# Routed gate and up products with the expert's weights as the stationary operand

## The reference, cut to what matters

```python
gu = einsum('th,ehf->etf', x, w_gate_up)      # per expert 512 -> 2 x 256
act = silu(gate) * up                         # 256
eo = einsum('eti,eih->eth', act, w_down)      # 256 -> 512
routed = einsum('te,eth->th', combine, eo)    # weights of the two chosen experts
```

## Time and profile before

| | us |
|---|---|
| median of 3 runs (range) | 1273.26 (1271.31 to 1275.28) |
| the profiled execution's own time | 1275.16 |
| its span from first to last instruction | 1273.4 |
| PE busy | 1205.0 (95%), mean granted clock 0.986 |
| PEld busy | 816.2 (64%) |
| DVE / ACT / POOL busy | 661.2 / 475.8 / 491.4 |
| DMA | 217.40 MB moved |

### The profile page before, as it was taken

The page is one execution under the profiler, slowest core; times in us unless marked ns, Lnnn a source line. Parts: engine busy times, 40 slices in busy tenths (PEclk is TensorE's granted clock), DMA queues, the critical chain, the costliest instruction groups (busy, mean ns, idle before and its releaser), DMA issues. The chain is left out here.

```text
span 1273.4 us, 29250 instructions
## 1 busy us (share of the span) xinstructions
PE 1205.0 (95%) x10768; PEld 816.2 (64%) x10768; DVE 661.2 (52%) x1410; ACT 475.8 (37%) x1030; POOL 491.4 (39%) x432
## 2 busy tenths in 40 slices
PE   3899999999999779999999899999999899999997
PEld 3666677677677457777777444444444477777775
DVE  7878888998988578633333222222222123333333
ACT  6455555555555362322222233333333311111111
POOL 3446656665675200445401122222222044444444
PEclk9999999999999889999999999999999999999999
DMA  6589888788778655344323687888889334444444
GB/s 207 129 220 216 196 214 247 200 222 236 207 222 238 197 199 181 95 109 96 104 100 45 165 194 191 188 196 185 193 193 186 97 133 150 149 149 148 149 149 133
DMA packets 269373, 217.40 MB, mean 171 GB/s; under 512 B 196784, under 2 KB 203056, under 8 KB 269296
## 3 DMA queue, kind: packets, MB, share of 16 engines
q1 hardware_dynamic: 255344, 180.03, 53.3%
q0 software_dynamic: 12848, 35.47, 9.8%
q10 hardware_dynamic: 1104, 0.81, 0.2%
HBM read 115.97 MB, written 56.51 MB: 135 GB/s over the span
## 5 line engine op out<-in xcount | busy, mean ns | idle before, releaser
L1434 PE MATMUL sc<-xT,WG 128*128 128x256 f16 x3072 | 348.9, 274 | 11.6 <-DVE WD L1730 8.4
L1434 PEld LDWEIGHTS sc<-xT,WG 128*128 128x128 f16 x3072 | 302.0, 98 | 61.7 <-DVE WD L1730 8.9
L1445 PE MATMUL sc<-WG,raw 128*128 x852 | 208.4, 381 | 5.4 <-DMA raw<-raw 3.2
L1869 DVE SCALAR_TENSOR_TENSOR actv<-sc,up_inv,sg 128x512 f32<-128x512 f32 x64 | 48.0, 751 | 246.1 <-ACT sg L1706 245.9
L1415 POOL DMA_INDIRECT raw<-xs_dram,slots x71 | 67.3, 948 | 280.2 <-DMA raw<-raw 208.3
L1706 ACT ACTIVATE sg<-sc,gate_inv 128x512 f32<-128x512 f32 x64 | 43.9, 687 | 303.3 <-PE sc L1434 300.8
L1452 PE MATMUL yp<-WD,ah 128*128 128x512 f16 x512 | 152.3, 379 | 1.4 <-DVE al L1874 1.4
L1445 PEld LDWEIGHTS sc<-WG,raw 128*128 128x128 f16 x852 | 83.7, 98 | 91.8 <-issue 8.8
L1937 POOL DMA_INDIRECT raw<-y_dram,gidx x64 | 64.3, 1004 | 151.8 <-DVE ys L1850 101.5
L791 PE MATMUL ring<-hT,qkvT 128*128 128x256 f16 x1024 | 120.9, 275 | 2.0 <-PEq L213 2.0
L2074 DVE TENSOR_TENSOR alr<-rat,ahr 128x256 f16<-128x256 f32 x71 | 30.2, 425 | 159.3 <-ACT ahr L2051 159.3
(11 more groups left out here) (260 smaller groups left out, 1776.4 us busy)
## 6 DMA issues: line engine op xcount, KB each, us to landing
y_dram<-raw SPq DMA_DIRECT2D x71, 256.0 KB
xl<-in_L_attn_x SPq DMA_DIRECT2D x16, 512.0 KB, 4.2
wraw<-in_L_ffn_w_gate_up SPq DMA_DIRECT2D x16, 512.0 KB, 4.6
xs_dram<-xs SPq DMA_DIRECT2D x16, 512.0 KB, 3.7
xT_dram<-x SPq DMA_DIRECT2D x16, 512.0 KB, 2.6
xr<-in_L_attn_x SPq DMA_DIRECT2D x16, 512.0 KB, 5.4
x_dram<-x SPq DMA_DIRECT2D x32, 256.0 KB, 2.1
xT<-xT_dram SPq DMA_DIRECT2D x16, 512.0 KB, 5.4
```

The costliest lines, as they stand in the source:

```text
L1434: ins = pe.matmul(gu[:, h, f * tokens:(f + 1) * tokens].rearrange("p (u t) -> p u t", u=B), w[:, kk, b, a0:a0 + P], x[:, :, a * KT + kk, : ...
L1445: ins = pe.matmul(gu[bank], x(kk, a), w[:, 0, kk, b, :], start=(i == 0), stop=(i == len(done) - 1))
L1869: v.scalar_tensor_tensor(out=actv[:, g % 2], in0=gu[g % 2][:, 1].rearrange("p (f t) -> p f t", f=FT), scalar=up_inv[:, 1:2], in1=sg[:], op ...
```

## The change

The expert's weights become the stationary operand, in four parts of 128 output channels; the activations are the moving operand with 128 columns. One tile takes 4 parts x 4 k-tiles x 3 passes = 48 matmuls of 128 columns into the same bank. The result has hidden channels on partitions and slots along the bank, the layout that the down product needs; so the two transposes, the bank `rat` and `at_full` go. The routing weight is no longer applied to `actv` (its slot would be a column now) but to the output rows, as the scale of ACT's output copy; `cw` is computed once for all tiles. PE now makes the whole product of tile r+1, then loads the next expert's number, then makes down of tile r. At the last tile the product of `shared(1)` is split around the last down product. On ACT the output copy of tile r-1 comes behind `ah` of tile r, and ACT no longer loops.

```diff
-        def gate_up_rows(pe, gu, bank, x, w, parts):
+        def gate_up_rows(pe, bank, x, w):
...
+            for part in range(2 * FT):
+                for kk in range(KT):
+                    for a, b in PASSES:
+                        ins = pe.matmul(bank[:, part * P:(part + 1) * P], w[:, 0, kk, b, part * P:(part + 1) * P],
+                                        x(kk, a), start=(kk == 0 and (a, b) == PASSES[0]),
+                                        stop=(kk == KT - 1 and (a, b) == PASSES[-1]))
...
-                        gate_up_rows(pe, gu_half, 0, slot_rows(0), WG[:, expert_of(pe, 0)], range(3 * KT)).then_inc(rows_full, 1)
+                        gate_up_rows(pe, gu_half[0], slot_rows(0), WG[:, expert_of(pe, 0)]).then_inc(rows_full, 1)
...
-                            gate_up_rows(pe, gu, 1 - par, slot_rows(r + 1), WG[:, nxt], FIRST)
-                        pe.wait_ge(S["act_ready"], r + 1)
-                        for f in range(FT):
-                            ins = pe.transpose(at[par][:, f, :], actv[:, par, f * P:(f + 1) * P], ident[:])
-                        ins.then_inc(S["at_full"], 1)
-                        if not last:
-                            gate_up_rows(pe, gu, 1 - par, slot_rows(r + 1), WG[:, nxt], REST).then_inc(S["gu_full"], 1)
+                            gate_up_rows(pe, gu[1 - par], slot_rows(r + 1), WG[:, nxt]).then_inc(S["gu_full"], 1)
                         else:
                             pe.wait_ge(x_ins[1][0], 16)
-                            gate_up(pe, gu_whole[0], xT[:, 0], WG[:, 0], B * P).then_inc(gu_fulls[1], 1)
+                            pe.wait_ge(S["act_ready"], r + 1)
+                            gate_up(pe, gu_whole[0], xT[:, 0], WG[:, 0], B * P, (0, 1))
...
                         down(pe, yp[par], (ah[:, par], al[:, par]), WD[:, own], True, True).then_inc(S["y_full"], 1)
+                        if last:
+                            gate_up(pe, gu_whole[0], xT[:, 0], WG[:, 0], B * P, (2, 3)).then_inc(gu_fulls[1], 1)
...
+                        act.activation(ysb[:, par], yp[par][:], ACT.Copy, scale=cw[:, r:r + 1]).then_inc(S["y_ready"], 1)
+
+                    for r in range(SLOT_TILES):
+                        par = r % 2
+                        act.wait_ge(S["gu_full"], r + 1)
+                        act.activation(sg[:, par], gu[par][:, 0:FFN].rearrange("p (f t) -> p f t", f=FT), ACT.Silu,
+                                       scale=gate_inv[:, 0:1]).then_inc(S["sg_ready"], 1)
+                        act.wait_ge(S["act_ready"], r + 1)
+                        act.activation(ah[:, par], actv[:, par], ACT.Copy).then_inc(S["ah_ready"], 1)
+                        if r > 0:
+                            y_evac(r - 1)
...
+                    v.tensor_scalar(cw[:], slots[:].bitcast(F32)[:, 0:SLOT_TILES, 1], out_inv[:, 0:1], None, ALU.mult
+                                    ).then_inc(S["cw_ready"], 1)
...
+                        v.scalar_tensor_tensor(out=actv[:, par],
+                                               in0=gu[par][:, FFN:2 * FFN].rearrange("p (f t) -> p f t", f=FT),
+                                               scalar=up_inv[:, 0:1], in1=sg[:, par],
+                                               op0=ALU.mult, op1=ALU.mult).then_inc(S["act_ready"], 1)
                         v.wait_ge(S["ah_ready"], r + 1)
-                        v.tensor_tensor(al[:, par], at[par][:], ah[:, par], ALU.subtract).then_inc(S["al_ready"], 1)
-                        v.wait_ge(S["act_ready"], r + 1)
-                        weight(q + 1, par)
+                        v.tensor_tensor(al[:, par], actv[:, par], ah[:, par], ALU.subtract).then_inc(S["al_ready"], 1)
```

More of the change, by code:

```diff
@@ L1424, in load_tokens, with gate_up @@
             sp.dma_start(x1[:, par], at_step(x1_steps, n)).then_inc(x1_ins[half][par], 16)
-        def gate_up(pe, gu, x, w, tokens):
+        def gate_up(pe, gu, x, w, tokens, parts=range(2 * FT)):
             for h in range(2):
                 for f in range(FT):
+                    if h * FT + f not in parts:
+                        continue
                     a0 = h * FFN + f * P
@@ L1455, in down @@
             return ins
-        FIRST, REST = range(0, 6), range(6, 3 * KT)
         SENDS = 4
@@ L1952, in routed @@
             with ExitStack() as c:
-                cw = sb(c, "cw", [P, 2])
-                sg = sb(c, "sgr", [P, 2, FFN])
-                actv = sb(c, "actvr", [P, 2, FFN])
+                cw = sb(c, "cw", [P, SLOT_TILES])
+                sg = sb(c, "sgr", [P, 2, FT, P])
+                actv = sb(c, "actvr", [P, 2, FT, P])
                 ah = sb(c, "ahr", [P, 2, FT, P], F16)
@@ L1959, in routed @@
                 gu = gu_half
-                at = [c.enter_context(nc.psum_tensor(f"rat{i}", [P, FT, P], F32)) for i in range(2)]
                 yp = [c.enter_context(nc.psum_tensor(f"ryp{i}", [P, DIM], F32)) for i in range(2)]
-                names = ("act_ready sg_ready at_full ah_ready al_ready y_full y_ready cw_ready sp_passed")
+                names = ("act_ready sg_ready ah_ready al_ready y_full y_ready cw_ready sp_passed")
                 S = {x: sem(c, "r_" + x) for x in names.split()}
@@ L2036, in _, with y_evac @@
                 def _(act):
-                    def y_evac(q, par):
-                        r = 2 * q + par
+                    def y_evac(r):
+                        par = r % 2
+                        act.wait_ge(S["cw_ready"], 1)
                         act.wait_ge(S["y_full"], r + 1)
-                        act.wait_ge(y_out[par], 16 * q)
-                        act.activation(ysb[:, par], yp[par][:], ACT.Copy, scale=out_inv[:, 0:1]).then_inc(S["y_ready"], 1)
+                        if r > 1:
+                            act.wait_ge(y_out[par], 16 * (r // 2))
+                        act.activation(ysb[:, par], yp[par][:], ACT.Copy, scale=cw[:, r:r + 1]).then_inc(S["y_ready"], 1)
@@ L2043, in step, with _ @@
+                    y_evac(SLOT_TILES - 1)
+                @block.vector
+                def _(v):
+                    v.tensor_scalar(cw[:], slots[:].bitcast(F32)[:, 0:SLOT_TILES, 1], out_inv[:, 0:1], None, ALU.mult
+                                    ).then_inc(S["cw_ready"], 1)
                     def step(q, par, first):
                         r = 2 * q + par
-                        act.wait_ge(S["gu_full"], r + 1)
-                        act.activation(sg[:, par], gu[par][:, 0:FFN], ACT.Silu, scale=gate_inv[:, 0:1]
-                                       ).then_inc(S["sg_ready"], 1)
@@ L2048, in step @@
[L2048 to L2069, removed]
@@ L2070, in step @@
                         v.wait_ge(S["sg_ready"], r + 1)
-                        v.scalar_tensor_tensor(out=actv[:, par], in0=gu[par][:, FFN:2 * FFN], scalar=cw[:, par:par + 1],
-                                               in1=sg[:, par], op0=ALU.mult, op1=ALU.mult).then_inc(S["act_ready"], 1)
+                        v.scalar_tensor_tensor(out=actv[:, par],
+                                               in0=gu[par][:, FFN:2 * FFN].rearrange("p (f t) -> p f t", f=FT),
+                                               scalar=up_inv[:, 0:1], in1=sg[:, par],
+                                               op0=ALU.mult, op1=ALU.mult).then_inc(S["act_ready"], 1)
```

## The result

| | before | after |
|---|---|---|
| median (range), us | 1273.26 (1271.31 to 1275.28) | 1387.49 (1383.0 to 1389.94) |
| profiled execution, us | 1275.16 | 1389.94 |
| PE / PEld busy, us | 1205.0 / 816.2 | 1264.5 / 936.8 |

The ratio is 1.0885, 95% interval 1.0858 to 1.0912: 9% slower, where 1358 us was forecast within 1331 to 1403. The difference of the medians is +114 us. The engine line of the page after, as the earlier trace rows: PE has more instructions and more busy time, and still a smaller share of the span.

The account below looks back on a forecast made before the run. PE's streaming bounded the kernel; after the change its sequencer would. 68 periods growing from 4.145 to 5.36 us (+82.6) plus small end terms gave +84.3 on 1275.16, so 1359.5, or 1358 us as median; range 1331 to 1403.

Parts of the forecast that it names:

- One computation for each different slice: PE's sequencer, routed tiles: one register computation per different weight slice, 32 + 4 a tile, 2272 on the gate/up line.
- The sequencer becomes the bound: Routed tile on PE: the sequencer's sum of 5.36 us exceeds 3.96 us of streaming, so address computation sets the period.
- Streaming of 3.96 us: PE's matmuls in one routed tile: 48 gate/up at 55.4 ns plus six down make 3.96 us, 0.15 below before.
- The price of a register-held stationary address: PE's weight loads with the address in a register: taken as nothing extra; at most +2.2 us for 48.
- The size of a period: Time between down products in the routed stage: 5.36 us instead of 4.145, +82.6 us over 68 periods.
- The pace: Time from one address computation to the next on PE's sequencer: 0.125 us, spread 0.114 to 0.143.
- The load: PE's sequencer loading the expert number with its checks, once a tile: 0.66 us.
- The ends: First and last of the routed tiles: first period about 7.1 us, +1.1; last tile -0.2 for two transposes less.
- Before the first down: Start of the routed stage: +0.4 us for tile 0's product and +0.4 us for tile 1's.
- The halved clock: Rival: PE's clock halves in the routed stage, +3.55 us a tile, 1518 us; chance 0.03.
- The faster rival: Rival: cheaper addresses hide, streaming stays the bound, each tile saves 0.15 us, 10.7 in all, 1262.5 us; chance 0.08.
- DMA share: Transfers in the routed stage: share falling from 0.80 to some 0.62.

Follow-up runs that it names:

- e5: Changed kernel with the expert number loaded for tile 1 only and kept in registers for all later tiles, addresses computed once: 1269.60 us, ratio to before 0.9978.
- e3: Kernel before, activations still stationary, each 512-column gate/up matmul cut into four of 128 columns: 1389.93 us, ratio to before 1.0931.
- e8: Changed kernel with the expert number loaded twice a tile, one load behind the other: 1449.28 us, ratio to before 1.1402.
- e1: Changed kernel with gate and up weights read at one fixed place; down and the number's load stay: 1268.20 us, ratio to before 0.9974.
- e7: Changed kernel with DVE copying each tile's gate/up weights into fixed buffers a tile ahead, number loaded behind down: 1267.40 us, ratio to before 0.9963.
- e4: Kernel before, each 512-column gate/up matmul made as two of 256 columns, 20 addresses a tile: 1272.16 us, ratio to before 1.0003.
- e9: Changed kernel with the fourth of four gate/up parts read from a fixed place, 28 addresses a tile: 1310.28 us, ratio to before 1.0299.
- e11: Changed kernel with the two up parts read from a fixed place, 20 addresses a tile: 1276.16 us, ratio to before 1.0034.
- e6: Changed kernel with the expert number loaded in the middle of the gate/up product instead of behind it: 1369.14 us, ratio to before 1.0770.
- e12: Changed kernel with the expert number loaded behind the down product: 1368.62 us, ratio to before 1.0753.
- e10: The copied-weights kernel e7 with every output tile stored a second time into an unread buffer: 1274.58 us, ratio to before 1.0025.

## Why the prediction was right, and where it was off

- **One computation for each different slice**: right, 2272, and e5 against the changed kernel shows that it is these that cost and not the use of registers as addresses.
- **The sequencer becomes the bound**: right. e3 reproduces the loss in the old arrangement, and the row over 4 to 36 addresses bends where the sum passes the streaming.
- **Streaming of 3.96 us**: right, 3.97 in e5. In the changed kernel itself the pattern one, two of the matmuls shows only from about the twentieth of a product on; the first come 56 ns apart, since the sequencer has worked ahead during down. The 81 ns that the Trainium skill's page "TensorE: Matmul & The Clock Gate" gives in "Back-to-back issue gap" does not hold here: 48 matmuls in a row with 48 weight loads ran at 56 ns.
- **The price of a register-held stationary address**: taken as nothing, and it is.
- **The size of a period**, 5.36 forecast, 5.87 measured: two terms of the sequencer's sum were too small. The pace: 0.125 us came from clean stretches; over a whole product it is 0.127 to 0.135, 0.131 in the mean, because nine in ten computations start 0.124 us after the last and the others up to 0.31, which at 36 a tile makes 0.2 us. "Every reading fits" was too much said: eight from 845.3 to 846.4 in the kernel before are 0.157 apart, with a longer gap in their middle, where the transposes stand. The kernel before has the same slower steps, in time that the sequencer had to spare. The load: 0.66 us was read from two loads of 0.31, and the stage of the kernel before has 0.30 too; in the changed kernel the record behind the product is 0.26 us longer in the mean (0.56), 0.30 in the median. By these, 36 x 0.131 + 0.92 + 0.2 = 5.84 of the 5.87 us. The kernel before gives little sign of it: single loads there take up to 0.66 us. 0.51 x 68 = 35 us.
- **The ends**: from the first period I expected +1.1 us; it is 9.12, +3.1, with 2.82 us of waiting for the turned rows. The last period shrank by 2.9 us (1130.28 - 1126.36 = 3.92 after 6.83), where I counted only the transposes: half of the static product went behind down, and the next block starts 4.72 us after down's start, nearly as before (4.67), so this half fell into a pause that PE had there anyway.
- **Before the first down**: +0.8 us forecast in two terms. From the first address of tile 0 to the first down product it is 10.4 us before (708.9 to 719.27) and 11.5 after (706.4 to 717.86), so +1.1. But the stage began 2.5 us earlier in the execution after, and so the first down came 1.4 us earlier. Over the traces of all kernels here it comes anywhere from 713.9 to 719.3 us, so this part is chance, and the sum could not have it.
- **The rivals.** The halved clock did not come (1.00), but in e8, with some 0.5 us more of idle time in a tile, the clock was 0.90. The faster rival's gain (0.15 us a tile) exists as streaming, but e1, e5 and e7 are only 2.3 to 4.1 us under the kernel before on the same chip (e5's 2.3 within the noise), of its 10.7: in e5 and e7 waits for turned rows return the rest, in e1 the load behind the product.
- **DMA share**: 0.62, as forecast.

Together 82.6 + 35 = 117.5 for the 68 periods, -2.9 and +3.1 at the ends, -1.4 before the stage and -1.5 behind it: 114.8 between the two profiled executions.

## What to carry to other kernels

An engine's sequencer has a budget of its own: before cutting instructions into smaller ones with run-time addresses, count the different addresses, multiply by the pace of the computations (not by their record's length), and compare with the engine's streaming time between them. As long as the sum stays below, they are free (20 a tile in e4), and above it each one costs nearly in full (0.12 us in e9). Then look at what the sequencer does in one piece, such as the load of a number: it must also fit under the matmuls that are handed out ahead of it, and 17 of 128 columns are 0.93 us (e1, e11). Where an idle engine can copy the chosen operand into a fixed place, the budget is freed (e7).

## What was not expected of the hardware

- The load of one register from SBUF on PE took 300 ns or 600 (medians) in kernels that differ only in its place (e6 and e12 against the changed kernel), and up to 709 in e10. The cause stays open.
- With fixed addresses PE's sequencer was 17 matmuls of 128 columns, 0.93 us, ahead when it came to its load, in e1 and e11 alike.
- The mean granted clock was 0.90 in the stage of e8, where PE paused 1.1 to 1.7 us before down in each tile, and 1.00 in the changed kernel with 0.4 to 1.2 us. The first seven periods of e8 had the long pauses too and still ran at 1.00.
- 56 ns a matmul with its own weight load holds for 48 in a row, also when the loads' addresses come from registers.
